# A megakernel of two layers on one core: another order of the lanes' steps on each engine

## What is computed

```
x = x + 0.5 * L0_ffn(layernorm(x))     # gated FFN 128 -> 352 -> 128, inputs and weights rounded to FP4
x = x +       L0_attn(layernorm(x))    # two Mamba layers: conv, softplus, selective scan over the tokens
x = x + 0.5 * L0_ffn(layernorm(x))
x = x + 0.5 * L1_ffn(layernorm(x))     # 8 experts 128 -> 512 -> 128, all computed, gates sigmoid > 0.5
x = x +       L1_attn(layernorm(x))    # 16 heads, causal, relative bias
x = x + 0.5 * L1_ffn(layernorm(x))

# the scan of a Mamba layer, for each of 256 channels and 16 states:
h = dA * h + dBx ;  y = sum over states of h * C
```

## Time and profile before

| | us |
|---|---|
| median of 3 runs (2762.08 to 2769.0) | 2767.91 |
| the profiled execution | 2769.06 |
| its span, first to last instruction | 2767.3 |
| TensorE busy | 2610.0 |
| VectorE busy | 1942.1 |
| ScalarE busy | 1605.7 |
| GpSimd busy | 1375.6 |
| line 1340, the fillers, on TensorE | 463.8 |

### The profile page before, as it was taken

The page is one execution under the profiler, slowest core; times in us unless marked ns, Lnnn a source line. Parts: engine busy times, 40 slices in busy tenths (PEclk is TensorE's granted clock), DMA queues, the critical chain, the costliest instruction groups (busy, mean ns, idle before and its releaser), DMA issues.

```text
span 2767.3 us, 41433 instructions
## 1 busy us (share of the span) xinstructions
PE 2610.0 (94%) x14847; PEld 1899.4 (69%) x14847; DVE 1942.1 (70%) x3753; ACT 1605.7 (58%) x3405; POOL 1375.6 (50%) x1227
## 2 busy tenths in 40 slices
PE   7999999998999889999899898989999999998998
PEld 7878875786687555776477566756676677667675
DVE  5979888797969786867849887788859766332310
ACT  1433437535665647756476566747675775565654
POOL 1458475573838364735617483574627536211011
PEclk9999999999999999999779899999999989999999
DMA  4223122231213120202102120211202122000000
GB/s 153 67 67 113 54 69 78 61 92 39 86 38 100 46 71 29 85 24 70 61 20 89 39 84 20 66 58 47 81 17 77 35 62 62 1 5 1 1 5 4
DMA packets 88572, 150.58 MB, mean 54 GB/s; under 512 B 10565, under 2 KB 21485, under 8 KB 88110
## 3 DMA queue, kind: packets, MB, share of 16 engines
q1 hardware_dynamic: 88366, 147.94, 17.6%
HBM read 145.26 MB, written 2.65 MB: 53 GB/s over the span
## 4 chain that ended last, share of the span: by engine, by line
PE 73%; DVE 12%; ACT 6%; issue 5%; POOL 4%; DMA 0%; POOLq 0%; SPq 0%; DVEq 0%; ACTq 0%
PE c_bank L913 15%; PE c_bank L921 15%; PE c_bank L1340 8%; PE a_bank L759 6%; PE b_bank L1073 3%; DVE hst L707 3%; PE b_bank L1062 3%; PE a_bank L749 3%; PE b_bank L1086 2%; PE b_bank L1085 2%; PE a_bank L728 2%; DVE a_bank L701 2%; POOL prod_c L830 1%; PE b_bank L581 1%; PE b_bank L1084 1%
## 5 line engine op out<-in xcount | busy, mean ns | idle before, releaser
L830 POOL TENSOR_TENSOR prod_c<-hst,prod_c 128x512 f32<-128x512 f32 x512 | 664.5, 1305 | 426.5 <-DVE hst L707 399.7
L707 DVE TENSOR_TENSOR_SCAN hst<-dA,a_bank 128x512 f32<-128x512 f32 x512 | 620.7, 1212 | 10.4 <-ACT dA L819 2.6
L819 ACT ACTIVATE dA<-delta,a_neg 128x510 f32<-128x510 f32 x512 | 365.3, 719 | 349.2 <-DVE hst L707 344.6
L913 PE MATMUL c_bank<-c_xT,w 128*128 128x512 f32 x1024 | 539.8, 631 | 13.7 <-ACT weighted_y L956 8.3
L921 PEld LDWEIGHTS c_bank<-w,hid 128*128 128x128 f32 x4096 | 494.5, 193 | 68.2 <-issue 31.3
L921 PE MATMUL c_bank<-w,hid 128*128 128x128 f32 x4096 | 517.5, 279 | 0.2
L1340 PEld LDWEIGHTS c_bank<-ident 128*128 128x128 f32 x3686 | 454.6, 194 | 46.5 <-issue 37.1
L1340 PE MATMUL c_bank<-ident 128*128 128x128 f32 x3686 | 463.8, 278 | 0.2 <-ACT weighted_y L956 0.2
L972 POOL TENSOR_TENSOR xs<-xs,weighted_y 128x512 f32<-128x512 f32 x128 | 169.4, 1323 | 556.5 <-ACT weighted_y L956 556.4
L948 ACT ACTIVATE hid<-c_bank,b 128x512 f32<-128x512 f32 x512 | 349.1, 687 | 148.6 <-PE c_bank L913 146.9
L701 DVE TENSOR_TENSOR a_bank<-du,a_bank 128x512 f32<-128x512 f32 x512 | 348.2, 680 | 46.5 <-PE a_bank L749 44.7
(11 more groups left out here) (180 smaller groups left out, 3573.1 us busy)
## 6 DMA issues: line engine op xcount, KB each, us to landing
prod_c<-c_rows SPq DMA_DIRECT2D x512, 256.0 KB, 3.2
w<-in_w SPq DMA_DIRECT2D x2, 2048.0 KB
xs<-in_x SPq DMA_DIRECT2D x8, 256.0 KB, 9.2
bias<-skew SPq DMA_DIRECT2D x1, 2048.0 KB, 8.2
out_dram<-xs SPq DMA_DIRECT2D x8, 256.0 KB, 2.3
in_wT<-in_in_wT SPq DMA_DIRECT2D x1, 512.0 KB
c_rows<-bcC SPq DMA_DIRECT2D x16, 32.0 KB, 1.6
b_hq<-in_w_gu SPq DMA_DIRECT2D x1, 384.0 KB, 3.1
```

What stands on the lines that cost most here:

```text
L707: nc.vector.tensor_tensor_scan(hst[:, s % RS, :], dA[:, s % RA, :], b_bank, 0.0, ALU.mult, ALU.add).then_inc(M.h.sem, 1)
L819: nc.scalar.activation(half_batches(dA[:, s % RA, :], 1), half_batches(delta[:, h, :], 1), ACT.Exp, scale=a_neg[:, l, h, n:n + 1]).then_in ...
L830: nc.gpsimd.tensor_tensor(prod[:, s % RP, :], hst[:, s % RS, :], cring[:, s % RC, :], ALU.mult).then_inc(M.pp.sem, 1)
L913: nc.tensor.matmul(S.bank[up_bank(e, c)][:, :], w1[:, e, c * 128:(c + 1) * 128], S.xT[:, :], start=True, stop=True).then_inc(M.up.sem, 1)
```

## The change

The five strings are replaced; nothing else is. They come from a planner that is not part of the kernel, which now lays a reserve on every handover from one engine to another when it works out which step goes where. What is in the strings, counted in steps:

| engine | steps | of them fillers, before and after | places that differ |
|---|---|---|---|
| TensorE | 4990, now 5386 | 1843, now 2239 | from the start on |
| VectorE | 3072 | none | 1008 |
| ScalarE | 3302 | none | 1418 |
| GpSimd | 1033 | none | 212 |
| SyncE | 538 | none | 10 |

The first line of TensorE's string:

```
-    "b2d8bd38bd3b2d6b2d6b2d28bd3b3d39b6d57aba3b2d9b2ad5ab2a2d9ad16bd12ab2d2bdad7ad27a2d3ad8adad4ad12a2d8ad14a2d10"
+    "b2d10bd55bd5b2d8b2d8b2d32bd5b3d43b5d2bd61adbda3b2d11b2ad7ab2a2d11ad17bd13adb2d3bd2ad8ad28a2d4ad9ad2ad5ad13a2"
```

More of the change, by code:

```diff
@@ new lines @@
+ORDER_ACT = (
+    "abab24a13ba3baba5ba10b3ab2a9b2ab2a83b4a8baba5ba4ba7b2ab3a12b2ab2a6b3aba7b2c2bc3bca4ca5b2cb3a3c3a2cac2a3ca10"
+    "b2c4ab2cac3ac4acac2aca3c5acac2a2c2ac3ac2aca2c4ac2ac2a2c4ac2ac2a2c3aca2c4a8b4a8baba5ba4ba7b2ab3a12b2ab2a6b3ab"
+    "a7b2c2bc3bca4ca4b2acb3a3c3a2cac2a3ca10b2c4ab2cac3a2c3ac2ac2ab3abcac6acb2ab2cbab2abc5acb2cacbacac4acb2ac2bac6"
+    "ab2cacbac4a2c4a4b24a4ba4b3a4b3ab3ab3ab3a4b4a3b4a2ba2ba6b4abab3a3b3a2b3a2b3a2b3a2b3a2b3a2b3a2b3ab3a2b3a2b3a2"
+    "b3ababab5c4a4ca4cabacacabcaca2c4bcbc5a3c2a2ba2bca6bab2c5ac2acac7acac4b2cbabc5b4c4ac2a2c7acac4bc4babac4acba2c"
+    "a7b2a2b3acacac3b4c4a8b4c2a4c3ab4cabab3a2ca2cba3b2a4ba5b2acac4b3ac8acb2acb2cab3ab3acb3c3ab3cab3cab3cab3acb3a"
+    "b3ab3ab3ab3cacb3c2acb3cab3cacb6ab3ab3ab3ab3cacb3c2acb3cab3cab3acb12cb3c3b2a4c2bca4ca4c3b4a3c2a3ca5ba2ba3caba"
+    "c4ac3acbac5ac3ac3ac3ab2c2ba2c8a2c7acac8ac5ac3a2c8b4ab2a2b4a6babc4bcbc2b5c8b4c8b4a4c2a4c3b4a4bcacb3a3b3cb3ab3"
+    "a2c7b2a3b2ca3b3ab3a2b3ab2abab3ac2ac3b3ab6ab2cabab3ca2b3cab3ab6ab3acb3c3ab3acb3ca2b3c2ab3ab6ab3ab3ac2b3c2b3a"
+    "b3ab3cacb3ab3cabcaba2bac7b4c6bcb2a4ca4bcac2a3c2b2c2abab2aca6c5a2c2acb2a2b2a3c6ac2b4c5ac3ac5acac2ba2bac5abac3"
+    "abac5ac2acac4ab2ab3ac4ac5a2cab2a2b2cacacb4c2a2c4b4c2bc3b3c2b3cb6c7b2ca2b2a4b3a2b2c3bc2a2b3ca2cb3ab3cb3a2b3a"
+    "b6a3b8aba2b3a2b3a2b3a2b3c2b3c3ab3c2a3b3cab3ab6c5ab3acb3acb3acb3ab3ab3ab3ab3c2bc2abacacacbacac4ab4ac4a2c5aca2"
+    "b2a2cbcbcacac4acac7b2cb3c8a4c2b2c2a3b2acac2a3b4ca3c5a2cacacaba2ba2c4bc2acbca3c5ac3ac2b2c2ab3ac4a2c4acacab2a"
+    "b2acac3ab4c2acac2ab4ac2bc3a2b3c2b2cbab2c4bc2b3c2ab2acb2c4ab3cab3cacb3ab3ab3ab3ab5c2bc2b3c2b3cb6cb12a4b3a4cb3"
+    "c4a3b3cacb3ab3cb3a2b3ab6a3b8aba2b3a2b3ac4ba2cbac2abca4c4b2c4b2ac4acaca2bcaba3bcacac2bcac3a2c6ac2ab3a2b2c5ac8"
+    "ac2acac2b2c2a2b2ac2ac2ab4ac7b4cbc4b3c2b2cbcb5aba3c4a4b2c4ab5a2c4b3cab3ab2cabab3a3b3a4b3cab3ab3ab2cbca2b3cac"
+    "b3acab3c2b3cab3ab3ac4abcb2acacb3ca2b3a2c3b2cbacabcb2acb3ca2b3a2c4acb3c2ab3acab3a2c2acb3cacab3cac2b6c2bc2bcb"
+    "c8b3cbc10b2c4bcbc4b2c2bc4b2c13b2c2b2c6b3cbc2b3cbc4bc2b2cb4c5b2cbc2b3c7b2cb5cb3c3b3cb3c3b6c2bcbcb3cb2cb5cb3c2"
+    "bcb2c2b3c2b3cb6c5b3c2b3cb3c2bcbcbc2b2cbcb6c4b2cbcb3c2b6c3bcb2c2b2cbcb3c2bc3bc3bc20b4c2b4cb4cb3c2b3c2b3c3b2c5"
+    "b2cb3c2b12cb3c4b3cb3cb3cb12cb3c4b3cb3cb3cb4c2bcbc2b3c2b3cb6c5b3c2b3cb4c2bcbc2b3c2b3cb4c2bc4bc73")
@@ new lines @@
+ORDER_POOL = (
+    "ab5a2b2a13ba86bab2a18ba12ba15ba2ca2b2aca4ca9ca6ca6ca6ca9ca3ca6bab2a18ba12ba15ba2ca2b2aca6baca3ba3ba3ca3ca6c"
+    "a4ca5ca2ca62bcabcba2ca4cabacabaca5ca2bac2aca14ba15ba2bab2caca2ca8ca14ca12ca11cac2b2a7ca3baca4ca3ca3caba3ca2c"
+    "aca3ba9baca7babcbababc2aca16ca13ca14cba2c2aba2bcbacba2ca4bca6ca7ca2baca4c2a6ba5ba5baba2ca3ca2c2a4ca12ca8bca3"
+    "c2a3ba13bca5cbacbcbcacba2ca4c2a5ba6ba4baba2ca5ca3ca11ca7c2abcac2a5ba15cba6ca3caba3ca4ba3cba2ba2ca3c3a7ca11c"
+    "a10ca12ca8cabcbc3bcbcbcb2c15b3c17")
@@ L119 @@
 ORDER_SP = (
[L120 removed]
+    "a248caca72caca64ca53ca56ca33c3")
 def merge(order, lanes, spare=None):
```

121 lines of the change are left out of this document (48 added, 73 removed).

## The result

| | before | after |
|---|---|---|
| median of the comparison, us | 2768.45 (2762.08 to 2771.17) | 2813.3 (2804.79 to 2819.93) |
| the profiled execution, us | 2769.06 | 2811.11 |
| its span, us | 2767.3 | 2809.3 |
| mean granted clock of TensorE | 0.955 | 0.960 |

The changed kernel takes 1.0174 times as long, 95% interval 1.0155 to 1.0192: slower by about 45 us (the two profiled executions differ by 42), against 54 forecast.

The account below looks back on a forecast made before the run. TensorE was taken to bound the kernel on paper, partly busy with unneeded fillers, with VectorE setting the pace in lane a's loops. 17 + 27 + 10 + 0 = 54 us on 2769.1, less 1.2 for the median: 2822 us (2766 to 2868).

Parts of the forecast that it names:

- loops of the first part: Lane a's loops up to the 225th L749: 178 added fillers, 42% of their time shows, 17 us (10 to 40).
- start and stretches between: Start and serial chains between lane a's loops, up to 225th L749: 138 added fillers cost 27 us (15 to 31).
- fillers of middle and end, and reordering: Behind the 225th L749: 80 added fillers cost 10 us (0 to 18); reordered lane work 0 (-30 to +30).
- (1): Line 1340, the filler, over the whole kernel: x4478, up by 88 us of back-to-back time.
- (2): Lane a's early loops: scan L707 spaced at 2.0 us instead of 1.85, VectorE idle before L701 because of L749.
- (3): The 225th L749 comes at 974 us (955 to 1001), from 930 before.
- (4): From the 225th L749 to the end: 1837 + 10 us.
- (5): At the start, L572 behind 32 and 43 fillers comes later by 0.9 us more each.
- The signs against it: 225th L749 below 950 us; later part over 30 us shorter with less waiting; or whole granted clock 0.97 and more.
- Only the loops pay: In the serial stretches up to the 225th L749, longer filler runs vanish in other waits: 2785 us, chance 0.15.
- The reserve pays: From 930.1 us on, TensorE waits less and regains clock: 55 us faster, 2713 us, chance 0.13.
- Fillers buy clock: Behind 930.1 us, 80 added fillers give back 51 us of lost clock: 2771 us, chance 0.08 including other near-zero endings.

Follow-up runs that it names:

- alone, with four fillers more: Kernel before with the change's fillers added only inside lane a's loops up to the 225th L749 (182 more): 2782.37 us, ratio 1.0074.
- the kernel with the rest of the change: Orders and fillers of before up to the 225th L749, those of the change from there on: 2772.92 us, ratio 1.0055.
- the one with the first part alone: All five orders and fillers of the change up to the 225th L749, those of before from there on: 2803.63 us, ratio 1.0150.
- the run with all but the loops: Kernel before with the change's fillers up to the 225th L749 only at the start and between lane a's loops (134 more): 2788.52 us, ratio 1.0089.
- three kernels: The kernel before, and it with the change's whole strings or only its fillers up to the 225th L749: the latter two 2803.63 and 2817.79 us.
- a fourth: Kernel before with the change's fillers only between lane a's sixth and seventh pass (49 for 31): 2776.21 us, ratio 1.0041.

## Why the prediction was right

It said slower, 2822 us (2766 to 2868); it is 2813.3. By its terms, from the two profiled executions, cut at the first and the last L749 of each pass:

| term | predicted, us | measured, us |
|---|---|---|
| loops of the first part | 17 (10 to 40) | 18.3; alone, with four fillers more, 20.4 |
| start and stretches between | 27 (15 to 31) | 21.4 (7.8 and 13.6); alone 24.6 |
| fillers of middle and end, and reordering | 10 + 0 | 2.3, from -28.1 and +30.4 |
| sum | 54 | 42.0 |

*Loops*: right in mechanism and size. VectorE set the pace, TensorE had 0.39 us to spare, and three fillers of 0.2234 used it up and 0.28 more. By the scans the same loops grew by 15.6 us (543.3 for 527.7).

*Start and stretches*: right in mechanism, 6 us too high. At the start, 7.8 us show of 51 fillers (11.4 us). In the stretches between, a typical one (272.3 to 316.3 us before) has 18 fillers more, 4.0 us, and is 2.4 us longer. My step of some 0.3 us of shelter for each handover was too small. Part of what was measured isn't of fillers at all: the stretch behind the seventh pass is 5.3 us longer by the scans (51.7 for 46.3), and it is 51.6 in the kernel with the rest of the change too, whose fillers are those of before up to the 225th L749, but 46.4 in the one with the first part alone. So that piece belongs to the reordering, and the fillers of this row cost some 16 us for my 27. I had not priced the clock either: in the stretch between the sixth and the seventh pass the traced change runs at 1.00 for 0.89, which pays 0.11 x 46.4 = 5 us; the same strings in the kernel with the first part ran it at 0.91, so this is not to be counted on.

*Middle and end*: 10 was forecast, 2.3 stand in the traces and some 15 in the ratio of the kernel with the rest of the change. The sum was near, but by luck: it is the difference of a middle 28 us shorter and an end 30 us longer, and neither was foreseen. I had weighed the reordering at 0, since the cover of L913 and L1073 did not grow. The runs without fillers show that the order alone is worth 23.5 us, within my bound of 30. The weak step is the measure: a count of the work between a matmul and its use doesn't see what the moved blocks do to the clock, where the rows of the runs without fillers put the gain. What hides the gain is in part that the fillers of before had bought it already. The end's +30.4 us is TensorE's busy time, +30.0: by the terms of the prediction 13.1 for the moved L913 and L921 and 1.3 for six fillers; by the clock, 0.06 x 463.1 - 0.04 x 432.7 = 10.5; some 5 remain for the 27 attention matmuls. This split is worked out and not tested by a run.

*The signs named ahead.* (1) x4478 and 557.3 us, +93.4 for +88. (2) The scans at 1.98 us spacing, with L749 as the releaser: yes. (3) The 225th L749 at 969.8 for 974. (4) The rest 1839.5 for 1847. (5) L572 later by 1.34 and 0.90 us more, forecast 0.9 each. The signs against it stayed away: 969.8 is far above 950, the later part isn't shorter, and the mean clock is 0.960, below the 0.97 named.

*The rivals.* "Only the loops pay" falls by the run with all but the loops. "The reserve pays" is true of the order (23.5 us) and not of the kernel. "Fillers buy clock" is true of the whole of the fillers (3.4%), and perhaps of the pass with 92 more: its clock is 0.85 in the earlier trace rows and 0.96 after, but it also has other work in it and takes 189.5 us for 160.6. Without any fillers that pass goes from 0.87 to 0.94 by the scans (289th to 321st), so the order does a good part of it. Over the later two parts the lost clock went from 101.6 to 0.05 x 1376.4 + 0.06 x 463.1 = 96.6 us only.

## What to carry to other kernels

Where an engine is kept awake by work that nobody needs, that work belongs between the end of one real step and the arrival of the next one's input, by a trace; a reserve for uncertain handovers may set the order of the real steps, and must not be turned into filler. Too much costs up to its own time, too little at one gap can cost several times that by the clock (12.6 us in the stretch above), and in that stretch the place mattered more than the sum. A change that is two changes (an order and its fillers) is judged only when each has run without the other.

## What the runs showed of the hardware

- A hole of 2.19 us in dense work of TensorE was followed by 24 us at a granted clock of 0.57, mostly at 1.2 GHz, though TensorE was busy for 22.6 of them (the row of 792 to 816 us above). With 0.18 us of waiting at the same place, the kernel before has a shorter fall some 3 us on, and 0.89 over the stretch. The stretch with the hole took 12.6 us more.
- With fillers of 128x128 in f32 with the unit matrix the clock stays at 1.00 over a stretch in which they are 70% of the time (32.7 of 46.4 us from 289.2 us on in the change). In the change's order without fillers the same stretch is at 0.71 and takes 48.25 us.
- The clock is not the same in two traces of the same instructions: one pass of lane a took 174.2 us at 0.82 in three kernels and 166.5 at 0.87 in a fourth, with the same strings from the 225th L749 on. Traces can't tell differences of a few microseconds in this kernel; repeated runs have to.
